# A DLRM kernel: the three columns that ScalarE fetched row by row are gathered by GpSimd

## What is computed

```python
h = relu(dense @ dw1 + db1); dense_emb = relu(h @ dw2 + db2)
sparse_emb = emb_tables[f_ids, sparse_idx]              # 2048 x 26 rows of 64 floats
emb = concatenate([dense_emb[:, None, :], sparse_emb], axis=1)   # 2048 x 27 x 64
inter = einsum('bfd,bgd->bfg', emb, emb)                # all pairs of features
z = concatenate([emb.reshape(B, -1), inter[:, iu0, iu1]], axis=1)
z = relu(z @ ow1 + ob1)                                  # 512 wide
z = relu(z @ ow2 + ob2); z = relu(z @ ow3 + ob3)         # 256, 128 wide
return z @ ow4 + ob4
```

## Time and profile before

| | |
|---|---|
| time, median of 3 runs | 532.94 us (532.85 to 534.67) |
| span of the profiled execution | 651.2 us |
| mean granted TensorE clock in it | 0.845 |
| PE busy | 489.1 us, 75% |
| GpSimd busy | 385.6 us, 59%, 406 gathers |
| ACT busy | 149.5 us, 23% |
| DVE busy | 154.8 us, 24% |

### The profile page before, as it was taken

The page is one execution under the profiler, slowest core; times in us unless marked ns, Lnnn a source line. Parts: engine busy times, 40 slices in busy tenths (PEclk is TensorE's granted clock), DMA queues, the critical chain, the costliest instruction groups (busy, mean ns, idle before and its releaser), DMA issues.

```text
span 651.2 us, 8430 instructions
## 1 busy us (share of the span) xinstructions
PE 489.1 (75%) x2262; PEld 259.7 (40%) x2262; DVE 154.8 (24%) x297; ACT 149.5 (23%) x337; POOL 385.6 (59%) x410
## 2 busy tenths in 40 slices
PE   6838857577695969867767887859767689796698
PEld 1314434243352535333333443424333244434577
DVE  1311303222122221402222131321212223041223
ACT  2212113121221303113130221312122131211323
POOL 6755656557566566656656666565656655663530
PEclk9967868779777988878897789789787799887799
DMA  8200010201011010110101011000100100100000
GB/s 264 67 21 24 23 24 22 60 22 26 19 24 23 23 23 24 24 23 22 24 22 25 21 25 23 20 23 22 25 21 24 23 22 21 26 23 11 22 17 3
DMA packets 19429, 19.56 MB, mean 30 GB/s; under 512 B 9760, under 2 KB 10787, under 8 KB 19369
## 3 DMA queue, kind: packets, MB, share of 16 engines
q0 software_dynamic: 12992, 13.33, 8.7%
q1 hardware_dynamic: 5202, 5.26, 2.6%
q10 hardware_dynamic: 1188, 0.44, 0.3%
HBM read 18.99 MB, written 0.01 MB: 29 GB/s over the span
## 4 chain that ended last, share of the span: by engine, by line
PE 29%; issue 25%; ACTq 13%; SPq 10%; another core or an unknown queue 10%; ACT 8%; DVE 4%; DMA 1%
ACTq L246 12%; SPq L246 9%; PE l_ps L771 8%; PE gram_ps L750 6%; PE l_ps L779 5%; PE tr_ps L803 3%; ACT gram_c L528 2%; ACT slots L516 1%; SPq L242 1%; ACT feat L508 1%; PE l_ps L866 1%; PE gram_ps L803 1%; PE gram_ps L866 1%; ACT pairs_b L540 1%
## 5 line engine op out<-in xcount | busy, mean ns | idle before, releaser
L304 POOL DMA_INDIRECT emb<-table_dram,rows x396 | 375.9, 949 | 235.9 <-issue 108.3
L771 PE MATMUL l_ps<-w_sb,feat 128*128 128x512 f32 x390 | 218.6, 714 | 71.6 <-ACT feat L508 69.7
L771 PEld LDWEIGHTS l_ps<-w_sb,feat 128*128 128x128 f32 x390 | 85.4, 229 | 188.2 <-issue 113.1
L383 DVE COPY gram_c<-gram_ps 32x432 f32<-32x432 f32 x60 | 36.6, 609 | 238.1 <-remote 131.2
L750 PE MATMUL gram_ps<-slots 64*128 64x108 f32 x960 | 72.0, 309 | 27.3 <-DVE gram_c L383 20.4
L750 PEld LDWEIGHTS gram_ps<-slots 64*128 64x128 f32 x960 | 66.3, 217 | 42.2 <-DVE gram_c L383 22.2
L528 ACT COPY gram_c<-gram_ps 32x432 f32<-32x432 f32 x60 | 30.5, 509 | 183.9 <-remote 106.0
L779 PE MATMUL l_ps<-w1p_sb,pairs 118*128 118x512 f32 x90 | 59.5, 813 | 10.0 <-issue 5.9
L350 DVE COPY feat<-tr_ps 128x512 f32<-128x512 f32 (+1 forms) x32 | 15.7, 492 | 166.2 <-remote 76.6
L508 ACT COPY feat<-tr_ps 128x512 f32<-128x512 f32 (+1 forms) x32 | 18.4, 575 | 151.7 <-issue 73.2
L516 ACT COPY slots<-tr_ps 64x256 f32<-64x256 f32 (+1 forms) x128 | 50.4, 394 | 1.1
(11 more groups left out here) (114 smaller groups left out, 225.4 us busy)
## 6 DMA issues: line engine op xcount, KB each, us to landing
own<-table_dram SPq DMA_DIRECT2D x896, 0.2 KB
emb<-table_dram,rows POOLq DMA_INDIRECT x396
own<-table_dram ACTq DMA_DIRECT2D x384, 0.2 KB
w_sb<-ow_dram SPq DMA_DIRECT2D x3, 1024.0 KB
w1p_sb<-ow_pairs_dram SPq DMA_DIRECT2D x1, 708.0 KB
w_sb<-ow_dram SPq DMA_DIRECT2D x1, 512.0 KB
w_sb<-ow_dram SPq DMA_DIRECT2D x1, 256.0 KB
idx_raw<-idx_dram ACTq DMA_DIRECT2D x1, 208.0 KB
```

The costliest lines, as they stand in the source:

```text
L304: pool.indirect_dma_start(out=pair_of(t, c // 2)[:, c % 2 * D:(c % 2 + 1) * D], out_offset=None, in_=table, in_offset=bass.IndirectOffsetO ...
L383: last = nc.vector.tensor_copy(dst, src)
L771: nc.tensor.matmul(l1_ps[t % 2][:], feat[t % 2][:, n - 1, :], w1_sb[:, n - 1, :], start=False, stop=False)
```

## The change

ScalarE fetches no rows. The tiles 6, 10 and 14 leave the list of own tiles, so their column 25 is gathered by GpSimd like any other. SyncE's seven tiles stay. The list of single rows that the host makes and VectorE turns into addresses shrinks from 1280 to 896 with `OWN`.

```diff
 SP_OWN = [2, 5, 7, 9, 11, 13, 15]
 HELD = 32
-ACT_OWN = [6, 10, 14]
-ACT_ROWS = 16
-OWN = SP_OWN + ACT_OWN
+OWN = SP_OWN
...
-            def fetch_some(i):
-                a, b = (min(x * ACT_ROWS, len(ACT_OWN) * P) for x in (i, i + 1))
-                if i == 0:
-                    act.wait_ge(own_rows, 1)
-                if a < b:
-                    fetch(act, mybir.EngineType.Activation, len(SP_OWN) * P + a, len(SP_OWN) * P + b)
-
...
                 for stage in mid_stages(t):
                     upper_act(*stage)
-                fetch_some(2 * t)
                 evac_features(t, 2)
                 group_slots(t, 2)
-                fetch_some(2 * t + 1)
```

## The result

The changed kernel takes **535.78 us** in the median (535.07 to 536.34, 5 runs) against 532.85 (532.31 to 534.67, 5 runs) for the kernel before beside it. The ratio is 1.0056, with an interval of 1.0043 to 1.0069. That is +0.56%, +2.93 us: slower, by just over what a measurement of this kernel can tell from no change. Forecast were +3.25 and 536.2. Repeated later on another chip the pair came to 534.66 against 532.47, 1.0043 [1.0029, 1.0058], +2.19 us.

What follows compares the result with a forecast made beforehand. The prediction took GpSimd's issue of gathers as the bound: 532.94 us plus 3.25 for three more gathers (2.5 in tiles 6 and 10, 0.75 in tile 14), all else 0, gives 536.2 us, with an 8-in-10 range of 532.5 to 538.0.

Steps and rivals of the forecast that it cites:

- GpSimd is the bound: Whole program: GpSimd's issue of gathers sets the time, 1.25 us each, 32.5 us a tile, with hardly a wait when timed.
- The two sums: Kernel before: trace without GpSimd's waits, 534.3 us; last gather plus landing and tail, 530.0; the median 532.94 lies between.
- The slow stretches are the recording: Profile of before: stretches with 700 ns row instructions and late semaphores come from recording; profiled execution 118.3 us over the median.
- Three gathers, +3.25: Column 25 of tiles 6, 10 and 14 on GpSimd: 2.5 us in full plus 0.75, ends +2.5 and +3.75.
- Tile 14's third gather, taken at 0.75: Tile 14, three upper-layer stages before transposes(14, 2): the gather costs between 0 and 1.25 us, taken as 0.75.
- VectorE's shorter passes, taken at 0: VectorE's four address passes, before TensorE's first transposition, work on 896 in place of 1280: 0 us.
- ScalarE's rows worth 0: Twelve tiles, 384 fewer rows: copy 1.0 us earlier, upper bound 15.6 us, worth 0 because TensorE waits for gathers anyway.
- SyncE's faster rows worth 0: SyncE's queue: keeps its rows, may issue a little faster; no one waits for it after tile 2, so 0.
- The gather is free for its issuer: Rival, GpSimd: dispatch about 50 ns by the skill page, so three gathers nearly free, 532.9 us; chance 0.03.
- Partly hidden: Rival: TensorE is later in places, two of three gathers cost, less up to about 2.5: 532.9 to 535.5 us; chance 0.28.
- ScalarE was the bound: Rival: unrecorded pitch is shorter, say 1.20 us, TensorE sets the pace with fetches on its path: 520 us; chance 0.07.
- More than the pitch: Rival, tiles 6 and 10: TensorE's longer wait may let its clock fall to half, +1.5 us allowed, 538; chance 0.06.

Runs made afterwards that it cites:

- rows kept: Changed kernel (409 gathers) with ScalarE still fetching its 384 rows into an unread spare buffer: 659.13 us, 1.0053 to before (long chip); 535.65 us, 1.0059 (quick chip).
- neither: Changed kernel with column 25 of tiles 6, 10 and 14 left as zeros, 406 gathers, no ScalarE rows: 645.91 us, 0.9888 to before (long chip).
- extra passes: Changed kernel with VectorE's address passes done three times more into spare buffers: 644.67 us, 0.9949 to before (long chip).
- twelve by rows: Twelve tiles' column 25 by single rows, nine SyncE's, three ScalarE's, 404 gathers: 736.31 us, 1.1248 to before (long chip); 530.62 us, 0.9971 (quick chip).
- the pair of runs made for it: Changed kernel with four more gathers into a spare buffer behind tile 8 (647.95 us, 1.0040 to before) or tile 14 (646.96 us, 1.0069), long chip.
- changed, again: The changed kernel unaltered, run again on the second, quick chip as base for the others: 534.66 us, 1.0043 to before.

## Why the prediction was right, point by point

**GpSimd is the bound: right.** It was read by taking GpSimd's 116.9 us of waits out of a trace that was 118 us too long. On quick chips those waits are not there, and five traces follow the count of gathers. The two sums by which it was checked were each less exact than they looked: neither had the 2.0 us around the span, and the lower one took 3.9 us for a landing of 2.6 and had no longer gathers. That the median lay between them was luck in part.

**The slow stretches are the recording: wrong.** This premise fell. They go with the chip: before takes 654 and 645 us there in its timed runs too. The conclusion survived because the waits do go with the stretches, and the median that was to be predicted came from a quick chip. That is luck in part: had it come from a long one, the sign would probably have been wrong. There, three gathers cost +3.5 us (rows kept) and 384 rows less give -7.3 (neither), together -3.8, and the changed kernel with the extra passes measures -3.3 us, 0.9949 [0.9906, 0.9992]. The changed kernel itself wasn't run on a long chip; by these runs I expect it some 0.5% faster than before there. The chain of before's trace, with 23% on the two row queues, was a true account of a long execution.

**Three gathers, +3.25: nearly right in the result, 1.1 us too high on the second chip.** On quick chips the difference is +2.93 and +2.19 us; the second lies under the sum's lower end of +2.5.

- *Tile 14's third gather, taken at 0.75: not refuted.* In the first trace of the changed kernel TensorE waits for the landing there and in the last tile (timeline of TensorE, after):

```profile
485.57 0.30 PE L701 MATMUL tr_ps<-ident_sb,emb 128*128 128x128 f32 x1 [0.64 <-DMA emb<-table_dram,rows]
...
515.49 0.44 PE L714 MATMUL tr_ps<-ident_sb,emb 128*128 128x128 f32 x2 [0.80 <-DMA emb<-table_dram,rows]
```

  The first of the two is for the very gather in question, and with 0.64 + 0.80 us of waits the gather can cost its full 1.25. In the second trace of the same kernel TensorE doesn't wait in tile 14, and little in the last:

```profile
515.26 0.44 PE L714 MATMUL tr_ps<-ident_sb,emb 128*128 128x128 f32 x2 [0.25 <-DMA emb<-table_dram,rows]
```

  Its last transposition comes 1.34 us behind this one, where twelve by rows, with the gather already there, has 1.11. So without the third gather TensorE could have ended 0.25 + 0.23 = 0.5 us earlier, hardly more. From the traces the gather is worth 0.5 in one execution and up to 1.25 in another, with 0.75 between them; the pair of runs made for it fell on a long chip.

- *VectorE's shorter passes, taken at 0: the mis-sized term.* In before's trace three gathers are longer while the passes run, timeline of GpSimd (start, us):

```profile
16.39 1.48 POOL L304 DMA_INDIRECT emb<-table_dram,rows  x1 [0.30 <-issue]
18.17 1.36 POOL L304 DMA_INDIRECT emb<-table_dram,rows  x1 [0.30 <-issue]
19.83 1.24 POOL L304 DMA_INDIRECT emb<-table_dram,rows  x1 [0.30 <-issue]
```

  That is 1.25 us, on the engine that sets the pace. In the first trace of the changed kernel none is longer (0.00), in the second two are (0.47). So, if before's timed executions are like its trace, the change gives back 0.8 to 1.25 us of its 3.75, and with 0.5 to 1.25 for tile 14 it comes to **+1.75 to +2.95**, where +2.93 and +2.19 were measured. This is worked out from traces; no run on a quick chip changed the passes alone. The rows were in the trace that the prediction was made from; it looked for passes that delay ScalarE or TensorE, and not at the gathers beside them.

- *The change from one quick chip to the next* is no larger than what the pitch can make, which takes one of two values in an execution: 1.2512 or 1.2484 in the two traces of the same changed kernel. Over 407 steps that is 1.1 us.

**ScalarE's rows worth 0: right** on a quick chip, but for another reason than was given. The prediction had ScalarE's copy 1.0 us earlier in each of twelve tiles and let TensorE's wait for gathers swallow it; its 2.11 and 1.12 were read in a long execution. With the rows kept on a quick chip the piece mostly ends before the transposition, and the copy follows by 0.67 us with and without fetches. There was nothing to swallow but in two tiles. The rows kept beside the gathers add 0.99 us. The trace is of the longest of those four executions (537.62 us, the others 535.17 to 535.94); it has no wait of GpSimd's, 1.64 us more of longer gathers than the changed kernel's of the same chip, and the longer of the two pitches, 1.1 us more.

**SyncE's faster rows worth 0: right** so far as the traces show. Its rows are not faster: 768 take 302.8 us in after and 302.9 with ScalarE's rows kept. They are done at 376.7 us, and the sum of the table has no place for them.

**The rivals.** *The gather is free for its issuer* is refuted: three cost +2.2 to +2.9 and nine +8.7 us. That was the rule taken from the Trainium skill, "DMA: Bandwidth & Descriptors", section "Anatomy of one DMA — SWDGE (gpsimd) path"; the measurement decides against it for gathers of 128 rows. *Partly hidden* rested on the 2.9 us between the lower sum and the median. They were the time around the span (2.0), the longer gathers (1.25) and 0.4 of pitch (1.2510 for 1.25), less 0.9 that the sum had too much behind the last gather. In the middle of the program nothing is hidden; in tile 14 part of a gather can be, as above. Its range, 532.9 to 535.5, does hold the second chip's 534.66. *ScalarE was the bound* fell with the pitch: it is 1.248 or 1.251 in every trace. *More than the pitch* didn't show: no difference on a quick chip is over the pitches. The granted clock is 0.92 over the whole span of the profiled execution.

## What to carry to other kernels

Before a wait is explained, the trace's span plus the time around it has to be compared with the timed median; where they differ by a fifth, both may be true, of two kinds of chip, and the same change can cost 1.6% on one and gain 1.4% on the other. Where one engine issues all the time, count its instructions and multiply by their pitch: a sum that closes to a microsecond leaves no room for the others' gains. And look beside each instruction on that engine for what makes it longer, since a pass on an idle engine that costs nobody a wait can still lengthen the path that way.

## What the runs showed of the hardware

- **A gather beside a pass of VectorE can be longer.** Of the gathers that start inside one of VectorE's passes over row addresses most take longer by 0.12 us less than what is left of it: 0.42 for 0.54 left (changed, again, 16.65), 0.52 for 0.64 (passes three times more, 23.07). Some take longer by all that is left: 1.11 for 1.09 (rows kept, 16.95), 0.41 for 0.38 (before, 18.17; line 338's pass ends at 18.55). Two that start in a pass's first 0.1 us take no longer at all, though 0.6 us of it is left: 10.10 in the first trace of the changed kernel, 10.14 in before. Where it starts just behind one, it takes 0.94: in the first trace of the changed kernel the gather at 17.61 follows this pass, which ends at 17.60:

```profile
16.52 1.08 DVE L336 SCALAR_TENSOR_TENSOR own_f<-own_raw,own_f 1x896 f32<-1x896 int32 x1
```

  So small shifts decide between 0 and 2.1 us in a whole run (column "longer by" of the table). Later in the program, where VectorE copies out of PSUM, no gather of the six traces discussed here is longer. The Trainium skill, "SBUF — State Buffer", section "Who interferes with whom", says that an instruction of VectorE in a two-port mode, or with two inputs in SBUF against one of GpSimd that reads SBUF, and GpSimd's shut each other out for the whole of whichever started first. The traces agree for the gather at 16.95 (1.11 for 1.09 of a pass with two inputs). They do not for the gathers at 10.10 and 10.14, which began in such a pass, nor for the gather at 15.32 of "rows kept", which started 0.39 before a pass and still took 0.38 more.
- **The pitch of gathers has two values**, near 1.248 and near 1.251 us. A trace keeps to one of them from 30 us to its end, to about 0.001, on quick and long chips alike.
- **Single rows have two prices.** A register move and a DMA are 29 and 228 ns or 700 and 699 ns. Where all are of the first kind, rows of twelve tiles are hidden; where many are of the second, SyncE needs 0.57 us a row in place of 0.39, and they cost 12%.
- **The copy that waits for TensorE** starts 0.05 us or 2.15 us behind the matmul's modelled end, at one place of the same kernel on a quick and a long chip; the matmuls themselves take 2.04 us in both.
